# Six-block network on one core: two expert steps in every slot, the accumulated rows read back earlier, joined gate and up tails, preparation ordered by arrival, maximum rows ahead of part loads

## What is computed

```python
x = x + 0.5 * ffn0(layernorm(x))      # f1: silu(gate) * up, hidden size 704, weights int32 less 128, times a scale per row
x = x + attn0(layernorm(x))           # a2: 16 heads of 16, rope, no mask
x = x + 0.5 * ffn0(layernorm(x))      # f3: as f1
x = x + 0.5 * mixture(layernorm(x))   # d4
x = x + attn1(layernorm(x))           # a5: 16 heads of 16, causal mask, ALiBi
x = x + 0.5 * mixture(layernorm(x))   # d6: as d4
```

```python
x = w_norm * xf * rsqrt(mean(xf * xf) + eps)
w_topk, sel = top_k(softmax(x @ w_router), 4)            # 32 experts, hidden size 176
# every expert takes its first 128 entries in order of (token, choice); later ones are dropped
y[e] = (silu(x[e] @ w_gate[e]) * (x[e] @ w_up[e])) @ w_down[e]
out  = sum of the chosen y times w_topk                  # added at the token's row
out += sigmoid(x @ w_shared_gate) * ((silu(x @ sw_gate) * (x @ sw_up)) @ sw_down)   # hidden size 704
return inp + out
```

## Time and profile before

| | us |
|---|---|
| median of 3 runs (2951.69 to 2960.51) | 2952.81 |
| the profiled execution | 2950.72 |
| its span in the trace | 2948.9 |
| PE busy in the span | 2667.6 (90%) |
| VectorE busy | 1946.6 (66%) |
| ScalarE busy | 1261.4 (43%) |
| GpSimd busy | 657.1 (22%) |
| moved by DMA | 175.78 MB, 60 GB/s |

### The profile page before, as it was taken

How to read it: one execution, slowest core, us unless ns; L and a number is a source line. 1 busy time by engine, 2 the same in 40 slices (tenths; PEclk the granted TensorE clock), 3 DMA queues, 4 the chain that set the end, 5 groups by cost and what they waited for, 6 DMA issues and landing times. The chain is left out here.

```text
span 2948.9 us, 40309 instructions
## 1 busy us (share of the span) xinstructions
PE 2667.6 (90%) x14292; PEld 1275.0 (43%) x14292; DVE 1946.6 (66%) x4227; ACT 1261.4 (43%) x1901; POOL 657.1 (22%) x640
## 2 busy tenths in 40 slices
PE   3987999999999999797999995999999999798997
PEld 2442233333333332354455663454544454455564
DVE  5877878777877885585774334767677674576333
ACT  1432456556655667443211221355455556221221
POOL 0554122131230300153002441222121100001341
PEclk8996899999999999998999997799999999899998
DMA  3004330321303300001202663633233430301566
GB/s 118 1 1 101 49 60 12 54 50 22 60 17 49 58 8 1 1 1 61 92 33 49 137 135 85 129 64 57 45 61 54 66 50 2 107 33 33 122 138 166
DMA packets 163075, 175.78 MB, mean 60 GB/s; under 512 B 19570, under 2 KB 136242, under 8 KB 162738
## 3 DMA queue, kind: packets, MB, share of 16 engines
q1 hardware_dynamic: 145348, 150.48, 22.9%
q0 software_dynamic: 12416, 17.84, 3.8%
q10 hardware_dynamic: 5120, 4.98, 0.5%
HBM read 116.32 MB, written 56.13 MB: 58 GB/s over the span
## 5 line engine op out<-in xcount | busy, mean ns | idle before, releaser
L1776 DVE TENSOR_REDUCE a_mx<-a_bank 128x1 f32<-128x512 f32 (+3 forms) x1792 | 1031.0, 627 | 285.3 <-PE a_bank L1517 219.0
L1653 ACT ACTIVATE a_E<-a_bank 128x1024 f32<-128x1024 f32 (+3 forms) x896 | 794.8, 932 | 477.5 <-PE a_bank L1574 328.3
L1517 PE MATMUL a_bank<-a_KT,a_QT 96*128 96x512 bf16 (+4 forms) x1792 | 597.0, 379 | 35.1 <-DVE a_mx L1776 25.2
L1574 PE MATMUL a_bank<-a_QT,a_KT 99*128 99x512 bf16 (+4 forms) x1792 | 510.7, 360 | 18.5 <-DMA a_QT<-a_mT 16.0
L1589 PE MATMUL a_bank<-a_E,a_Vg 128*32 128x512 f32 (+3 forms) x3584 | 442.3, 566 | 0.7 <-ACT a_E L1653 0.7
L1517 PEld LDWEIGHTS a_bank<-a_KT,a_QT 96*128 96x128 bf16 (+1 forms) x1792 | 152.2, 98 | 526.1 <-DVE a_mx L1776 305.6
L1574 PEld LDWEIGHTS a_bank<-a_QT,a_KT 99*128 99x128 bf16 (+1 forms) x1792 | 170.4, 99 | 199.0 <-ACT a_E L1653 37.0
L848 PE MATMUL d_bank<-wdT,d_hT 128*128 128x256 f32 (+1 forms) x768 | 201.9, 407 | 21.7 <-DVE x L1054 21.7
L960 ACT ACTIVATE d_silu<-d_bank 128x512 f32<-128x512 f32 x96 | 57.2, 596 | 375.6 <-PE d_bank L835 368.4
L1044 DVE SCALAR_TENSOR_TENSOR d_silu<-d_silu,d_bank 128x512 f32<-128x512 f32 x96 | 65.6, 683 | 227.3 <-ACT d_silu L960 219.9
L433 POOL TENSOR_TENSOR f_hl<-f_hT,f_hh 128x512 f16<-128x512 f32 x96 | 111.1, 1157 | 392.1 <-ACT f_hh L452 392.1
(11 more groups left out here) (234 smaller groups left out, 3537.8 us busy)
## 6 DMA issues: line engine op xcount, KB each, us to landing
parts<-a_parts SPq DMA_DIRECT2D x64, 384.0 KB, 2.5
a_QT<-parts SPq DMA_DIRECT2D x180, 128.0 KB, 5.4
a_KT<-parts SPq DMA_DIRECT2D x180, 128.0 KB, 8.0
d_wgu<-in_L_ffn_w_gate SPq DMA_DIRECT2D x64, 176.0 KB
d_wgu<-in_L_ffn_w_up SPq DMA_DIRECT2D x64, 176.0 KB
d_wd<-in_L_ffn_w_down SPq DMA_DIRECT2D x64, 176.0 KB
normalised<-d_xn SPq DMA_DIRECT2D x8, 1152.0 KB, 4.7
acc<-d_zero SPq DMA_DIRECT2D x66, 128.0 KB, 1.8
```

The lines of the kernel that those rows point to most:

```text
L1517: last = nc.tensor.matmul(out[:, 0:w], QT[0:W, h, qt * P:(qt + 1) * P], KT[0:W, h, kh * HALF:kh * HALF + w], start=True, stop=not diag)
L1574: last = nc.tensor.matmul(out, KT[:, h, kt * P:(kt + 1) * P], QT[:, h, half * HALF + c0:(half + 1) * HALF], start=True, stop=not diag)
L1653: nc.scalar.activation(E[:, u % 2, 2 * pair:2 * pair + 2, c0:HALF], bank[:, 2 * pair:2 * pair + 2, c0:HALF], ACT.Exp).then_inc(exps, 1)
L1776: nc.vector.tensor_reduce(mx[:, j, qt, kh:kh + 1], out[:, 0:w], AX.X, ALU.max).then_inc(freed_dve, 1)
```

## The change

1. **Preparation.** x of batches 2 and 3 is loaded by SyncE after the weights and scales; the attention weights are loaded ahead of the scales. Gate, up and down weights have a semaphore each. VectorE converts each of them as it arrives and takes statistics and copies between; PE waits for the conversion that its group needs.
2. **Tails.** The tail blocks of gate and up (64 columns each) are put side by side into one block of 128 (`ctT` in the dense phases, `wtT` in the mixture) and multiplied in one product into gate's bank; the up half stands in partitions 64 to 127 and is read from there by the hidden step.
3. **Root table.** `core.want_root()`, a Sqrt activation on one column, stands at the end of ScalarE's stream in preparation, dense phases, attention, and in d4.
4. **START = 0** in mixture and attention: their semaphores are not raised.
5. **Mixture.** Two expert steps in every slot: 27 to 44. Finishes in slots 46 (0, 1), 47 (2), 48, 49, 50, 51, 52 (3 to 7). In the last chunk the down products alternate between banks 4 and 5. The first `gate_up` stands before `route_logits(0)` and waits for six weight DMAs; transposes of the first tiles go to banks 4 to 7. One DMA zeroes `acc`. In d4 statistics of batch 0 alone are taken; those of batches 1 to 3, with a second root on ScalarE, are in the opening of a5.
6. **Attention.** Maxima are made for five units' worth of chunks ahead in a5 (a2: four as before). A part load is due no earlier than three units after the maxima step, behind the maximum rows.

The diff, cut to its core:

```diff
+FM = (FB - 1) * P
+FR = FF - FM
...
+    def want_root(self):
+        self.nc.scalar.activation(self.rooted[:], self.eps[:, 0:1], ACT.Sqrt)
...
-def scope(core, ctx):
+def scope(core, ctx, start=START):
...
-    def sem(name, start=START):
+    def sem(name, start=start):
...
@@ prepare_phase: SyncE, ScalarE @@
+                for q, a, came in (("L0_ffn_wq_gate", qg, qg_in), ("L0_ffn_wq_up", qu, qu_in)):
...
+                sp.dma_start(qd[:], dram["L0_ffn_wq_down"].rearrange("(k p) f -> p k f", p=P)).then_inc(qd_in, 16)
+                for w, name in enumerate(("L0_attn_wq", "L0_attn_wk", "L0_attn_wv", "L0_attn_wo")):
...
+                for b in (2, 3):
+                    sp.dma_start(core.x[:, b * TPB:(b + 1) * TPB, :],
...
-                for b in range(B):
+                for b in (0, 1):
...
@@ prepare_phase: VectorE @@
-                for t in range(NT):
-                    if t % TPB == 0:
-                        dve.wait_ge(x_in[t // TPB], START + 16)
-                    nc.vector.bn_stats(bn[:, t, :], core.x[:, t, :]).then_inc(bned, 1)
-                dve.wait_ge(q_in, START + 16 * 5)
...
+                dve.wait_ge(qg_in, START + 32)
+                for j in range(FB):
+                    r = hid(j)
+                    nc.vector.tensor_scalar(fg[0:r, j, :], qg[0:r, j, :], ZERO_POINT, None, ALU.subtract).then_inc(deq, 1)
+                keep(0)
+                dve.wait_ge(qu_in, START + 32)
...
+                keep(2)
+                statistics(0)
+                dve.wait_ge(qd_in, START + 16)
...
+                keep(4)
+                keep(6)
+                keep(8)
+                statistics(1)
+                keep(10)
+                keep(12)
...
+                statistics(2)
+                statistics(3)
...
-                        pe.wait_ge(deq, START + 2 * FB + KC)
+                        pe.wait_ge(deq, START + (FB if 4 * n < KC * FB else 2 * FB if 4 * n < 2 * KC * FB else 2 * FB + KC))
...
@@ ffn0_phase: gate_up, hidden @@
-                    for w, acc in ((core.cgT, gate), (core.cuT, up)):
+                    for w, acc in ((core.cgT, gate), (core.cuT, up)) if j < FB - 1 else ((core.ctT, gate),):
...
-                                                   in1=up[0:r, j % 2, :], op0=ALU.mult, op1=ALU.mult).then_inc(h_ready, 1)
+                                                   in1=up[:, j % 2, :] if j < FB - 1 else gate[FR:P, j % 2, :],
+                                                   op0=ALU.mult, op1=ALU.mult).then_inc(h_ready, 1)
...
+                core.want_root()
...
@@ mixture_phase @@
+    START = 0
...
-        k = min(2 - (n % 3 == 0), NE + LAG - step)
+        k = min(2, NE + LAG - step)
...
-        finishes.setdefault(min(max(n + 2 + q // 3, (q + 1) * FB + CT), len(slots) - 1), []).append(q)
...
+    finishes = {slots[n]: qs for n, qs in ((len(slots) - 7, (0, 1)), (len(slots) - 6, (2,)), (len(slots) - 5, (3,)),
+                                           (len(slots) - 4, (4,)), (len(slots) - 3, (5,)), (len(slots) - 2, (6,)), (len(slots) - 1, (7,)))}
...
-        return 4
+        return 4 + i % 2 if c == NCH - 1 else 4
...
-                for q in range(NT + 1):
-                    sp.dma_start(acc[q * P:(q + 1) * P, :], zero[:, 0:D]).then_inc(zeroed, 16)
+                sp.dma_start(acc.rearrange("(q p) d -> p q d", p=P), spread(zero[:, 0:D], 1, NT + 1)).then_inc(zeroed, 16)
...
-                    for w, out in ((core.wgT, bank[:, acc_bank(n), :]), (core.wuT, bank[:, 2 + acc_bank(n), :])):
+                    gate, up = bank[:, acc_bank(n), :], bank[:, 2 + acc_bank(n), :]
+                    for w, out in ((core.wgT, gate), (core.wuT, up)) if j < FB - 1 else ((core.wtT, gate),):
...
-                        pe.wait_ge(x_done, START + t - (1 if down_bank(c, i) != down_bank(c, i - 1) and i else 0))
+                        pe.wait_ge(x_done, START + t - (1 if i and down_bank(c, i) != down_bank(c, i - 1) else 0))
+                    if down_bank(c, i) == 5:
+                        pe.wait_ge(y_s, START + NE)
...
-                route_logits(0)
                 if load:
-                    pe.wait_ge(w_in, START + 64)
+                    pe.wait_ge(w_in, START + 96)
...
-                    if j == 0 and 0 < c < NS:
+                    if j == 0 and c < NS:
                         route_logits(c)
...
+                if not final:
+                    core.want_root()
...
-                    if not final:
+                    if q < TPB // CT and not final:
...
-                    dve.wait_ge(stats, START + NCH)
-                    for t in range(NT):
+                    dve.wait_ge(stats, START + TPB // CT)
+                    for t in range(TPB):
                         nc.vector.bn_aggr(core.mv[:, t, :], bn[:, t, :])
...
@@ attention_phase @@
+    START = 0
...
-    AHEAD = 4 * C // U
+    AHEAD = (5 if second else 4) * C // U
...
-                        todo.append((max(G * U + u + 5, ((b - 1) * NG + g + 1) * U), load, (b, g)))
+                        todo.append((max(G * U + u + 5, ((b - 1) * NG + g + 1) * U, G * U + m_unit + 3), load, (b, g)))
...
                 load_first(act, 1)
+                if second:
+                    act.wait_ge(known_rest, START + 1)
+                    nc.scalar.activation(core.rstd[:, TPB:NT], core.mv[:, TPB:NT, 1], ACT.Sqrt, bias=core.eps[:, 0:1]).then_inc(root_rest, 1)
                 for x in rest_of[0 if second else 4:]:
                     take(x)
...
                 lower(3)
+                if second:
+                    for t in range(TPB, NT):
+                        last = nc.vector.bn_stats(bnr[:, t - TPB, :], core.x[:, t, :])
+                    last.then_inc(stats_rest, 1)
+                    dve.wait_ge(stats_rest, START + 1)
+                    for t in range(TPB, NT):
+                        last = nc.vector.bn_aggr(core.mv[:, t, :], bnr[:, t - TPB, :])
+                    last.then_inc(known_rest, 1)
...
+                    if second and G == 0:
+                        dve.wait_ge(root_rest, START + 1)
+                        nc.vector.reciprocal(core.rstd[:, TPB:NT], core.rstd[:, TPB:NT]).then_inc(scales, 1)
+                        dve.wait_ge(scales, START + 2)
```

More of the change, by code:

```diff
@@ L602, in mixture_phase @@
     LAST = n - 1
-    finishes = {}
-    for q in range(NCH):
-        finishes.setdefault(min(max(n + 2 + q // 3, (q + 1) * FB + CT), len(slots) - 1), []).append(q)
-    finishes = {slots[n]: qs for n, qs in finishes.items()}
+    finishes = {slots[n]: qs for n, qs in ((len(slots) - 7, (0, 1)), (len(slots) - 6, (2,)), (len(slots) - 5, (3,)),
+                                           (len(slots) - 4, (4,)), (len(slots) - 3, (5,)), (len(slots) - 2, (6,)), (len(slots) - 1, (7,)))}
     def acc_bank(n):
@@ L1619, in _ @@
             def _(act):
-                nc.scalar.activation(core.rstd[:], core.mv[:, :, 1], ACT.Sqrt, bias=core.eps[:, 0:1]).then_inc(root, 1)
+                nc.scalar.activation(core.rstd[:, 0:known], core.mv[:, 0:known, 1], ACT.Sqrt, bias=core.eps[:, 0:1]).then_inc(root, 1)
                 def take(x):
```

88 lines of the change are left out of this document (52 added, 36 removed).

## The result

The changed kernel takes 2877.3 us in the median of 4 runs (2868.2 to 2882.3), the kernel before 2954.4 (4 runs): a ratio of 0.9733, 95% interval 0.9703 to 0.9762. The profiled execution is the fastest of the four, 2868.24 with a span of 2866.5 against 2948.9, 82.5 us less. A second set of 4 runs of the changed kernel, beside other experiments, gave a median of 2871.8.

What follows compares the result with a forecast made beforehand. PE was taken to bound the middle of each phase, and a chain crossing engines the seams. The terms summed to -85.9 us from 2950.7, giving 2864.8, plus one for the timed runs: 2866, range 2840 to 2895.

Steps and rivals of the forecast that it cites:

- a5's opening: Start of a5: statistics of batches 1 to 3 and a wait on ScalarE delay the first chunk; cost 5.9 us, ends 0 and 8.
- the ends of d4 and d6: Mixture ends: three slots' dense work comes behind the last expert product; gains 17.1 us in d4, 14.6 in d6.
- dense tails: f1 and f3: joined tails only lengthen PE's wait for xl, except in the last chunk; gain 1.7 us, other end 13.8.
- a5's chunks: a5: five units of chunks ahead remove 8 waits of 9.2 us, at a cost of 1.0; gain 8.2 us, ends 4 and 9.
- The table load: Seams: an early root moves ScalarE's Sqrt table load into idle time; 1.28 us at f1, a2, f3 and d6, 5.1 in all.
- (d): Rival: dense tails pay in full (12 us more) and drains go with the tables (5.5): 2848 us; chance 0.12.
- The 8.8: a2: maximum rows ahead of part loads remove three PE waits, 3.58 + 3.33 + 1.89 us; gain 8.8, 5 at least.
- the order of the router's product: Mixture heads: first gate and up ahead of the router's product; d6 gains 1.1 us, d4 loses 1.7.
- the denser steps: Mixture: two expert steps in every slot cost 4.6 us a phase, 9.2 in both; ends 0 and 50.
- (a): Rival: the scatter chain bounds the expert slots, 6.1 us a scatter, 48 us in both mixture phases: 2914 us; chance 0.12.
- (b): Rival: weight loads stretch the scatter chain until the kernel is slower than before, from 6.7 us a scatter; chance 0.03.
- (c): Rival: START and table savings at the seams are zero, half the tails are lost to the routing chain: 2894 us; chance 0.10.

## Why the prediction was right or wrong

The measured 2877 lies 11 us above the forecast and inside the range. Preparation, START, a5's opening and the ends of d4 and d6 came by the mechanism that was given. The dense tails and a5's chunks did not, 22 us together, and luck covered a part of it: d6 gave 9 us more than forecast, by terms that were mis-sized.

**Preparation and seams: right.** Preparation gave 11.5 us (forecast 11.0), START 11.8 (11.0). The table load is seen alone at the seam of a2 and f3, whose semaphores are raised as before: 3.40 to 2.12 us, 1.28. The seams gained 3.5 more than the sum counted; 2.7 of it is the load in front of d4 and a5, which the sum had left out as hidden. In d4 it is hidden, as forecast: SyncE's first issue comes 1.66 us ahead of the reciprocal before and 0.38 after, the weights come as much later by the reciprocal, and PE waits for them. In a5 the way from the reciprocal to the first chunk took 34.4 us before and 34.3 with the root later, so there the load's time was gained. The Trainium skill (Advanced Engine Details and Errata, DMA Bandwidth Details) gives an increment about 1 cycle, in a list on DMA; for these instructions on SyncE the measured 0.061 us each decides. The Trainium skill (ScalarE: Activation LUTs, What ACT_TABLE_LOAD costs) would give 2.66 a switch; the seam gained 1.28.

**Dense tails: the failed step.** "The saving only lengthens that wait" was right, and its price was taken as nothing. The wait went from 1.3 to 2.1 us, and in four chunks of each phase PE then ran 3.4 us at half clock. The two kernels with more work on PE and less time show that. The bounds given, 1.7 to 13.8 of gain, excluded a loss with no reason, so 13.1 us of the miss are here. Rival (d) went the other way.

**a5's chunks: the failed step.** Two things. The 9.2 us of the earlier trace rows is a sum of PEld's waits, the weight loads; PE itself waited 6.4. And those 6.4, once gone, were not gained, as PE then waited on the maxima and in short pieces. The sum missed by 9.0. The comparison with four units shows 5.1 us for the fifth, in an execution with three more stretches at half clock, which can cost as much.

**a2: right in mechanism, mis-sized.** The 8.8 were the waits of the trace, and the stretches at half clock behind them were left out: up to 5.1 more. 13.7 were gained, and 20.2 lost in the undoing.

**a5's opening: right.** 5.9 forecast, 6.2 measured, by the wait that the prediction named; moving the root took it back.

**The mixture.** The end of d4 went as worked out from T, now 1734.0, where the last expert product ends. These lines answer to the earlier trace rows:

```profile
1732.83 1.13 PE L929 MATMUL d_bank<-d_wd,d_e_hT 88*128 88x256 f32 x4
...
1737.86 1.55 POOL L801 DMA_INDIRECT acc<-d_ys,d_index  x1 [3.05 <-DMA acc<-d_ys,d_index]
...
1747.11 1.22 DVE L1207 TENSOR_TENSOR x<-x,d_xn 128x1024 f32<-128x1024 f32 x1
...
1753.69 14.47 PE L888 MATMUL d_bank<-wdT,d_hT 128*128 128x256 f32 x48 [5.18 <-DVE d_hT L1088]
...
1769.99 0.63 DVE L1257 BATCH_NORM_AGGREGATE mv<-d_bn 128x2 f32<-128x6 f32 x8
```

The finishes start at T + 13.1 (forecast 13.3), PE goes on at T + 19.7 (20.1), the phase ends at T + 36.7 (36.2). The last scatter is issued at T + 3.9, earlier than the T + 6 to 9 given. In d6 the span ends at T + 34.2, not 36 (and T before was 2914.6 by the earlier trace rows, not 2914.4). Most of the rest of d6's extra 8.9 lies at its head: the order of the router's product was priced at 1.1, and undoing it cost 7.3. The step that failed there is that it counted PE's wait and not at which clock the router's 32 matmuls run. For d4 the forecast was a loss of 1.7; the undoing gave 1.7 back, within the spread. The tails were worth 30.7 in the undoing instead of 24.1, and the denser steps cost nothing that is seen instead of 9.2.

**Rivals.** (a) and (b) fell, but not by a wide margin. The 32 scatters of d4 are issued over 164.2 us (1573.66 to 1737.86), 5.3 apart, where they were 5.8 apart before (180.9 us). The sign that the prediction named did show: intervals up to 6.8 us, and VectorE waiting for a landed scatter. This is the view of waits from 1573 to 1734 in the changed kernel:

```profile
DVE d_ys L1200 <- DMA acc<-d_ys,d_index: 12.2, 6, 2.7
```

Before there was one such wait, of 1.45 us. PE waited for that product of VectorE 0.2 us in all (1.4 before), so the chain of scatters isn't the bound; it now runs at about PE's pace. (c) fell with the semaphores. (d) went the other way in the tails. What would have caught the errors is a rival that wasn't there: the clock. It gave in d6, where the granted clock rose from 0.94 to 0.97, and took in f1 and f3.

## What to carry to other kernels

Price a wait on PE by what follows it as well as by its length: look at the distance between starts behind it. Where another engine bounds a stretch, as VectorE does in f1, taking work off PE only makes it stand still longer; give it something to do in the wait (matmuls whose operands are there already) or leave it alone. Here small matmuls belonged behind large ones, where the operands of the large ones were there (d6, not d4). And when a wait is added to an engine's stream, put it after everything that doesn't need it. Take waits from the engine that bounds, not from the row of its weight loads.

## What the runs showed of the hardware

- The clock behind a wait: in f1 and f3, from their second chunk on, the seven waits for xl of each phase are 1.75 to 2.5 us in the changed kernel, and four of the seven were followed by half clock, for about 3.4 us, which cost up to 1.7. The first of the seven, 2.28 us, was not, though it is the longest of f1. In the kernel before and with split tails they are 0.9 to 1.6 us, and none was. The same code took 171.4, 171.5, 172.9, 173.1 (twice), 173.3, 176.2, 177.2 and 177.7 us in f1 in nine traces.
- The same waits of 1.7 us in a5 were followed by full clock in one kernel and by half clock in another, so a wait's length alone doesn't tell.
- The router's 32 small matmuls took 7.03 us in front of the first gate and up of d6, at half clock, and 3.65 behind them.
- Reading a product from partitions 64 to 127 of a bank into partitions 0 to 63 took VectorE 0.75 us for 512 columns (at 107.39 in the changed kernel), the same as a block of 128 partitions read in place (104.03).
- A semaphore increment on SyncE ahead of a barrier cost 0.061 us: 192 of them, 11.8 us.
